# Moving the normalisation of the layer norms before the first feed-forward layer and the second attention from GpSimd to VectorE

## The reference

```
x = x + tanh(g_xattn[0]) * L0_xattn(layernorm(x), ctx, ...)   # 16 heads of 64
x = x + tanh(g_ffn[0])   * L0_ffn(layernorm(x), ...)          # 8 gated experts, dense
x = x + tanh(g_xattn[1]) * L1_xattn(layernorm(x), ctx, ...)   # 16 heads of 16
x = x + tanh(g_ffn[1])   * L1_ffn(layernorm(x), ...)          # top-2 of 8, only where routed
def _layernorm(x, eps=1e-05):
    m, v = mean(x, -1), var(x, -1)
    return (x - m) / sqrt(v + eps)
```

## Time and profile before

| | |
|---|---|
| median of 3 runs | 3753.66 us (3750.41 to 3754.77) |
| profiled execution, its own time | 3753.66 us |
| its span, first to last instruction | 3751.7 us |
| PE matmul busy | 3675.7 us (98% of the span) |
| DVE busy | 2420.4 us (65%) |
| ACT busy | 1707.0 us (46%) |
| POOL busy | 1508.2 us (40%) |
| granted TensorE clock, mean | 0.997 of full |
| POOL, normalising (L552) | 139.4 us in 256 instructions |
| DVE, y_minus (L1193) | 25.6 us in 128 instructions |

### The profile page before, as it was taken

The page is one execution under the profiler, slowest core; times in us unless marked ns, Lnnn a source line. Parts: engine busy times, 40 slices in busy tenths (PEclk is TensorE's granted clock), DMA queues, the critical chain, the costliest instruction groups (busy, mean ns, idle before and its releaser), DMA issues.

```text
span 3751.7 us, 96179 instructions
## 1 busy us (share of the span) xinstructions
PE 3675.7 (98%) x34836; PEld 2990.3 (80%) x34836; DVE 2420.4 (65%) x5566; ACT 1707.0 (46%) x3115; POOL 1508.2 (40%) x1589
## 2 busy tenths in 40 slices
PE   7999999999999999999999999999999999999998
PEld 5878878878878878878878878878878878878865
DVE  4566666666666666666666666666666666666675
ACT  4444444444444444444444444444444444444431
POOL 3434434434434434434434434434434434434433
PEclk9999999999999999999999999999999999999999
DMA  3000000000000000000000000000000000000001
GB/s 96 11 14 16 11 14 16 11 14 16 11 14 16 11 14 16 11 14 16 11 14 16 11 14 16 11 14 16 11 14 16 11 14 16 11 14 16 11 27 64
DMA packets 58916, 64.83 MB, mean 17 GB/s; under 512 B 5344, under 2 KB 55808, under 8 KB 58240
## 3 DMA queue, kind: packets, MB, share of 16 engines
q10 hardware_dynamic: 34688, 32.52, 2.9%
q1 hardware_dynamic: 24192, 31.81, 2.6%
HBM read 47.01 MB, written 17.30 MB: 17 GB/s over the span
## 4 chain that ended last, share of the span: by engine, by line
PE 77%; POOL 7%; DVE 7%; issue 5%; ACT 2%; POOLq 1%; DVEq 1%; SPq 0%; DMA 0%; ACTq 0%
PE g L834 24%; PE g L840 13%; PE scores L834 10%; PE g L987 6%; PE scores L937 6%; POOL q_lo L608 4%; PE g L1006 3%; PE g L903 3%; PE scores L997 3%; DVE y_nm L1269 3%; POOL kmx L601 2%; PE g L854 2%; PE scores L971 2%; PE scores L941 2%; PE g L914 1%
## 5 line engine op out<-in xcount | busy, mean ns | idle before, releaser
L777 ACT ACTIVATE prob<-scores 120x1024 f32<-120x1024 f32 x512 | 499.6, 1026 | 481.0 <-PE scores L941 444.1
L1330 DVE SCALAR_TENSOR_TENSOR x<-g,lg_w,x 128x256 f32<-128x256 f32 x1024 | 494.5, 483 | 259.9 <-PE g L834 236.1
L834 PE MATMUL g<-ew_hi,yT_hi 128*128 128x512 f32 x1024 | 428.1, 418 | 0.0
L543 POOL TENSOR_TENSOR y_rstd<-y_mv,eps 128x2 f32<-128x2 f32 x128 | 24.9, 195 | 970.5 <-DVE y_mv L1188 970.5
L613 POOL TENSOR_TENSOR q_lo<-an,q_hi 128x512 fp32r<-128x512 f32 x256 | 326.6, 1286 | 210.3 <-ACT q_hi L806 210.3
L834 PE MATMUL g<-ew_lo,yT_hi 128*128 128x512 f32 x1024 | 404.7, 395 | 0.0
L834 PE MATMUL g<-ew_hi,yT_lo 128*128 128x512 f32 x1024 | 404.1, 395 | 0.0
L1269 DVE TENSOR_REDUCE y_nm<-g 128x4 f32<-128x480 f32 x512 | 301.1, 651 | 110.1 <-PE g L914 110.1
L1269 DVE TENSOR_REDUCE x_nm<-g 128x4 f32<-128x480 f32 x512 | 312.4, 653 | 72.3 <-PE g L903 72.3
L543 POOL TENSOR_TENSOR x_rstd<-x_mv,eps 128x2 f32<-128x2 f32 x64 | 12.5, 196 | 835.7 <-DVE x_mv L1188 835.7
L608 POOL TENSOR_TENSOR q_lo<-q_full,q_hi 128x512 fp32r<-128x512 f32 x256 | 324.9, 1291 | 1.1 <-ACT q_full L711 1.1
(11 more groups left out here) (214 smaller groups left out, 9437.2 us busy)
## 6 DMA issues: line engine op xcount, KB each, us to landing
x_in<-in_x ACTq DMA_DIRECT2D x64, 256.0 KB, 2.9
out<-y_x SPq DMA_DIRECT2D x64, 256.0 KB, 2.1
ctx_in<-in_ctx ACTq DMA_DIRECT2D x128, 120.0 KB, 2.4
wk_s<-in_gu SPq DMA_DIRECT2D x8, 512.0 KB, 4.0
vx<-in_ew SPq DMA_DIRECT2D x2, 1024.0 KB, 5.0
wk_s<-in_wk SPq DMA_DIRECT2D x1, 1024.0 KB, 5.2
prob<-in_wq SPq DMA_DIRECT2D x1, 1024.0 KB, 7.7
wv_s<-in_wv SPq DMA_DIRECT2D x1, 1024.0 KB, 10.3
```

The source lines that it names most:

```text
L777: a.activation(prob[:, e].rearrange("p o u s -> p (o u s)"), scores[0:NK, banks, :].rearrange("p o c -> p (o c)"), ACT.Exp, scale=scale).t ...
L834: ins = t_.matmul(out_, lhsT[u], rhs[v], start=first and n == 1, stop=last and n == 3 * len(terms))
L1330: ins = v.scalar_tensor_tensor(out=x1[:, t, :], in0=ring.bank(Y_FFN[j])[:, o * D:(o + 1) * D], scalar=lg_w[:, t, 2 * n + o:2 * n + o + 1], ...
```

## The change

The two normalisations of the y family leave POOL. POOL keeps only add and power. DVE no longer computes y_minus (nor the drain before it), and two new DVE steps take over: p_norm, placed after y_maxt 1 and before n_q 2, and y_norm3, placed in the loop after x_mul 1 and before x_mul 2. Both wait for POOL's root and issue two tensor_scalar instructions (subtract mean, multiply by root), with the function that the next batch's layer norm uses. POOL's waits for the ring (that the earlier transposes of xn are over) go away; on DVE the order of its own steps covers them.

```
@@ ORDER (the ENDS lists get the same two steps in like places)
-    ("x_mul", 2), ("x_mul", 3), ("x_pv", 1), ("x_pv", 2), ("x_hi", 1), ("x_sum", 1), ("x_pv", 3),
+    ("y_norm3", 0), ("x_mul", 2), ("x_mul", 3), ("x_pv", 1), ("x_pv", 2), ("x_hi", 1), ("x_sum", 1), ("x_pv", 3),
-    ("y_maxt", 0), ("n_q", 0), ("n_k", 1), ("n_q", 1), ("y_maxt", 1), ("n_q", 2), ("p_load", 0),
+    ("y_maxt", 0), ("n_q", 0), ("n_k", 1), ("n_q", 1), ("y_maxt", 1), ("p_norm", 0), ("n_q", 2), ("p_load", 0),
@@ GpSimd
-            def rstd(mv, rs, stats, k_stats, done, k, i, minus=False):
+            def rstd(mv, rs, stats, k_stats, done, k, i):
-                if minus:
-                    stats.wait(pool, i, k_stats + 1)
-            def normalise():
-                pool.drain()
-                for t in range(T):
-                    ins = g.tensor_scalar(xn[:, t, :], x1[:, t, :], y_minus[:, t:t + 1], y_rstd[:, 1, t:t + 1],
-                                          ALU.add, ALU.mult)
-                ins.then_inc(y_normed.sem, 1)
             def y_norm2(i, _):
-                if not first(i):
-                    ring.full(pool, i - 1, Y_TR3)
-                rstd(y_mv, y_rstd, y_stats, 2, y_rs, 0, i, minus=True)
-                normalise()
+                rstd(y_mv, y_rstd, y_stats, 2, y_rs, 0, i)
             def y_stat3(i, _):
-                if not (isinstance(i, int) and i + 2 >= B):
-                    ring.full(pool, i + 2, X_TR)
-                rstd(y_mv, y_rstd, y_stats, 5, y_rs, 2, i, minus=True)
-                normalise()
+                rstd(y_mv, y_rstd, y_stats, 4, y_rs, 2, i)
@@ VectorE
-            def minus_mean():
-                dve.drain()
-                v.tensor_scalar(y_minus[:], y_mv[:, :, 0], -1.0, None, ALU.mult).then_inc(y_stats.sem, 1)
             def p_stat(i, _):
                 x_made.wait(dve, i, 1)
                 statistics(x1, y_st6, y_mv, y_stats)
-                minus_mean()
+            def p_norm(i, _):
+                y_rs.wait(dve, i, 2)
+                normalise(x1, y_mv, y_rstd, xn, y_normed)
             def y_stat3(i, _):
                 ring.all_empty(dve, i, Y_FFN[6:8])
                 statistics(x1, y_st6, y_mv, y_stats)
-                minus_mean()
+            def y_norm3(i, _):
+                y_rs.wait(dve, i, 4)
+                normalise(x1, y_mv, y_rstd, xn, y_normed)
```

More of the change, by code:

```diff
@@ L72 @@
         ("x_mul", 2), ("x_mul", 3), ("x_pv", 2), ("x_hi", 2), ("x_hi", 3), ("x_pv", 3), ("n_k", 0), ("n_tr", 0),
-        ("n_k", 1), ("x_out", 0), ("x_out", 1), ("x_out", 2), ("x_out", 3), ("p_stat", 0), ("n_q", 0),
+        ("n_k", 1), ("x_out", 0), ("x_out", 1), ("x_out", 2), ("x_out", 3), ("p_stat", 0), ("n_q", 0), ("p_norm", 0),
         ("n_q", 1), ("n_q", 2), ("p_tr2", 0), ("p_load", 0), ("n_q", 3), ("n_res", 0), ("n_max", 0), ("p_gate", 0),
@@ L80 @@
         ("x_st", 2), ("y_ffn", 3), ("n_norm", 0), ("y_ffn", 4), ("y_ffn", 5), ("y_ffn", 6), ("y_ffn", 7),
-        ("y_stat3", 0), ("n_tr", 0), ("x_pv", 0), ("x_sum", 0), ("x_mul", 0), ("x_st", 3), ("x_pv", 1),
+        ("y_stat3", 0), ("n_tr", 0), ("x_pv", 0), ("x_sum", 0), ("y_norm3", 0), ("x_mul", 0), ("x_st", 3), ("x_pv", 1),
         ("x_mul", 1), ("x_hi", 0), ("x_mul", 2), ("x_hi", 1), ("x_mul", 3), ("y_res", 0), ("x_sum", 1), ("x_pv", 2),
@@ L84 @@
         ("n_k", 0), ("n_v", 0), ("x_out", 0), ("y_max", 0), ("x_out", 1), ("x_out", 2), ("y_max", 1), ("x_out", 3),
-        ("p_stat", 0), ("n_q", 0), ("y_maxt", 0), ("n_k", 1), ("n_q", 1), ("y_maxt", 1), ("n_q", 2),
+        ("p_stat", 0), ("n_q", 0), ("y_maxt", 0), ("n_k", 1), ("n_q", 1), ("y_maxt", 1), ("n_q", 2), ("p_norm", 0),
         ("p_tr2", 0), ("n_q", 3), ("y_st", 0), ("n_max", 0), ("p_gate", 0), ("n_max", 1), ("y_st", 1), ("n_max", 2),
@@ L93 @@
         ("x_st", 2), ("y_ffn", 6), ("y_ffn", 7), ("y_stat3", 0), ("x_sum", 0), ("x_st", 3), ("x_pv", 0), ("m_coef", 2),
-        ("x_mul", 0), ("x_hi", 0), ("x_pv", 1), ("x_mul", 1), ("x_sum", 1), ("x_pv", 2), ("m_norm", 0),
+        ("x_mul", 0), ("x_hi", 0), ("x_pv", 1), ("x_mul", 1), ("x_sum", 1), ("x_pv", 2), ("m_norm", 0), ("y_norm3", 0),
         ("x_hi", 1), ("x_pv", 3), ("m_coef", 3), ("x_mul", 2), ("x_mul", 3), ("m_tr", 0), ("y_tr3", 0), ("z_out", 0),
@@ L97 @@
         ("y_res", 0), ("x_out", 1), ("x_out", 2), ("y_max", 1), ("x_out", 3), ("p_load", 0), ("p_stat", 0),
-        ("m_bias", 0), ("m_gu", 0), ("y_v", 0), ("p_ctx", 0), ("y_maxt", 0), ("y_maxt", 1), ("p_tr2", 0),
+        ("m_bias", 0), ("m_gu", 0), ("y_v", 0), ("p_ctx", 0), ("y_maxt", 0), ("y_maxt", 1), ("p_norm", 0), ("p_tr2", 0),
         ("p_gate", 0), ("y_st", 0), ("p_lg", 0), ("m_gu", 1), ("y_st", 1), ("y_mul", 0), ("y_pv", 0), ("p_wt", 0),
@@ L103 @@
         ("m_sig", 0), ("y_ffn", 0), ("y_ffn", 1), ("z_hi", 1), ("y_k", 0), ("y_ffn", 2), ("y_ffn", 3), ("m_sig", 1),
-        ("y_ffn", 4), ("y_ffn", 5), ("y_ffn", 6), ("y_ffn", 7), ("y_stat3", 0), ("m_gu", 2),
+        ("y_ffn", 4), ("y_ffn", 5), ("y_ffn", 6), ("y_ffn", 7), ("y_stat3", 0), ("y_norm3", 0), ("m_gu", 2),
         ("y_tr3", 0), ("m_sig", 2), ("z_out", 0), ("y_v", 0), ("m_dnw", 1), ("m_gu", 3), ("m_dnw", 0), ("y_q", 0),
@@ L312, in flamingo_stack @@
         y_st6, y_mv, y_rstd = sb("y_st6", [P, T, 6]), sb("y_mv", [P, T, 2]), sb("y_rstd", [P, 2, T])
-        y_minus = sb("y_minus", [P, T])
         yT = pair("yT", [P, KD, S])
@@ L356, in flamingo_stack @@
         x_attn_hi, x_attn_lo = signal("x_attn_hi", QUADS), signal("x_attn_lo", QUADS)
-        y_stats, y_rs, y_resd, y_normed = (signal("y_stats", 6), signal("y_rs", 4), signal("y_resd"),
+        y_stats, y_rs, y_resd, y_normed = (signal("y_stats", 4), signal("y_rs", 4), signal("y_resd"),
                                            signal("y_normed", 2))
@@ L1420, in m_gate_up @@
                 v.tensor_scalar(m_u[n % 2], m_u[n % 2], -LIMIT, 1.0, ALU.max, ALU.add).then_inc(m_up, 1)
-            run(dve, {"n_stat": n_stat, "n_norm": n_norm, "p_stat": p_stat, "y_stat3": y_stat3,
-                      "n_tr": x_tr, "n_k": x_k,
+            run(dve, {"n_stat": n_stat, "n_norm": n_norm, "p_stat": p_stat, "p_norm": p_norm, "y_stat3": y_stat3,
+                      "y_norm3": y_norm3, "n_tr": x_tr, "n_k": x_k,
                       "x_mul": x_mul, "y_mul": y_mul, "p_tr2": y_tr(Y_TR2, 1), "y_tr3": y_tr(Y_TR3, 3), "y_k": y_k, "y_q": y_q,
```

## The result

The changed kernel takes 3773.61 us (median of 4 runs, 3770.41 to 3775.9), the kernel before 3752.47 us (4 runs, 3750.41 to 3754.77): 1.0053 of the time before, interval 1.0041 to 1.0066. It is slower by 21 us, where 3728 was forecast. The span of the profiled execution grew from 3751.7 to 3772.6 us at a granted clock of 0.996, against 0.997.

What follows compares the result with a forecast made beforehand. PE's own stream was taken to bound the kernel, so only its stalls counted: 17.4 us (n_max 1) + 7.2 us (y_q) + 1 us (ends) = 25.6 us off 3753.66 us, giving 3728 us, range 3718 to 3748.

Steps and rivals of the forecast that it cites:

- the part on the lock: DVE and POOL exclude each other; L1197's 406 ns at half L1420's width taken as a slower mode, speaking for no contention.
- DVE, added: Two tensor_scalar per norm on DVE, at most 0.81 us a pair, none on PE's path; counted as 0 us.
- this rival: Lock, slower: p_norm held by q_lo 0 and kmx, PE stands 1.1 to 1.4 us at p_tr2; 3820 us, chance 0.08.
- signs of being wrong: A spread like L1420's, PE's transposes of xn waiting for DVE, or no turn shorter by 0.4 us though both waits are gone.
- p_stat, POOL: q_lo 0 starts 1.3 us earlier on POOL, so PE's 0.29 us stall at n_max 1 goes; worth 17.4 us.
- y_stat3, POOL: POOL's low halves come earlier, so yT_lo is ready and PE's 0.12 us stall at y_q goes; worth 7.2 us.
- Margin 0.7 us: At both y_norm3 and p_norm, xn would be ready on DVE 0.7 us before PE's transposes read it.
- the work of y_minus and the ring waits: Removing DVE's y_minus (25.6 us in 128) and drain, and POOL's ring waits, counted as nothing.
- The ends: First and last batches, where PE waited for xn itself: 2 us gained to 2 us lost, taken as 1 us gained.

Runs made afterwards that it cites:

- e6: The kernel before, with only n_norm of the x family cut into pieces of 128, 128, 64 and 192 columns instead of two of 256; 3751.85 us.
- e3: The changed kernel with p_norm put directly behind p_stat on DVE, ahead of kT_lo; 3805.41 us, 1.0141 of the kernel before.
- e4: The changed kernel with POOL waiting after each of the two roots until DVE has finished the norm; 3766.8 us, 1.0038 of the kernel before.
- e5: The changed kernel with p_norm directly behind p_stat and POOL waiting after each root for DVE's norm; 3721.96 us, 0.9919 of the kernel before.
- e7: The changed kernel with p_norm directly behind p_stat and POOL waiting for p_norm alone; 3716.2 us, 0.9909 of the kernel before.
- e1: The kernel before with only the norm of y_stat3 moved to DVE (y_norm3); 3742.82 us, 0.9974 of the kernel before.
- e8: The kernel before with only p_norm moved to DVE, directly behind p_stat, and POOL waiting for it; 3732.7 us, 0.9949 of the kernel before.
- e2: The kernel before with only p_norm moved to DVE, at the change's place; 3790.53 us, 1.0099 of the kernel before.
- e9: As e7, with y_norm3 one x_mul earlier, between x_mul 0 and x_mul 1; 3730.14 us, 0.9942 of the kernel before.

## Why the prediction failed

*The step that failed* is in the part on the lock: L1197 "looks like an instruction of another, slower mode", because it is half as wide as L1420 and takes nearly as long. In the sum this is the term "DVE, added", which put the new instructions at 0.81 us a pair and "none of it on PE's path": 0 us. Measured, it is 60 x 0.93 us at p_tr2 and 60 x 0.15 us at y_tr3, 65 us. A rate was read from one duration each. e6 shows that two thirds of these 406 ns are fixed and that the slope allows L1197 the rate of L1420's best. So the comparison of durations spoke neither for nor against the lock; L1420's spread, which was for the lock, should have decided, and with it the fact that p_norm was moved to where POOL has q_lo 0 and kmx without a break. A chance of 0.08 for this rival was much too low. That L1197 is free of the lock "is not shown" stood in the same paragraph. Two of the signs of being wrong that the prediction names came: a spread like L1420's, and PE waiting for DVE's xn.

*The lock.* In the Trainium skill (SBUF — State Buffer, Who interferes with whom) the rule is that whoever comes first has the shared ports for its whole instruction and the other is blocked; e3 agrees, where POOL is first by 0.07 us and the DVE pair takes 3.17 us instead of 0.74, and so does the change, where the first instruction of y_norm3 is ahead of q_lo by 0.22 us and takes its 0.40. How far POOL is blocked when it comes second is not settled: that q_lo begins 0.19 us before the norm's end and takes only 0.05 us more. In e4 and e5 the two never meet, and all norms take 402 to 417 ns. The same section says that an instruction with at most one input in SBUF, outside the modes that use both port pairs, does not contend; kT_lo agrees, with 0.66 us beside q_lo 0. No run here shows the ports themselves, only that the engines exclude each other for these two kinds of instruction.

*The size of that rival.* It had PE standing 1.1 to 1.4 us at p_tr2, 3820 us. The transposes came 0.93 us late. As it says, the first instruction gets in at the end of q_lo 0 and the second waits for kmx; but it let xn be ready 0.5 us or more after kmx (1876.3 against 1875.8), and it is 0.15 us. It spoke of p_norm alone; y_norm3 was held too, for 0.15 us a turn. And it credited the change with only 0.12 us a turn, though both stalls went: 0.60, and 0.19 elsewhere. Its condition, a delay of more than 1.1 us, was met: p_norm's pair took 1.57 us longer than the 0.74 us of an undisturbed one.

*p_stat, POOL.* Right. The stall at n_max 1 went from 0.494 to 0.204, 0.29 us, forecast 0.29, and ACT's wait for POOL disappeared.

*y_stat3, POOL.* Right in kind, wrong in size. The step to y_q fell by 0.31 us, not 0.12. I had taken 0.21 us, the distance from a score matmul to the maxima, for the distance between context transposes and y_q; unhindered it is 0.026.

*DVE, added.* "a pair takes at most 0.81 us": wrong at both places, 1.70 and 2.31 us, and right once POOL waits, 0.72 to 0.74 us. "Margin 0.7 us" was used up at both: 0.15 us late at y_tr3, 0.93 at p_tr2. Taking away the work of y_minus and the ring waits showed no cost of its own.

*The ends.* I had 1 us of gain. In the change the time before and after the turns grew by some 4 us (20.9 us of span, less 57 to 60 turns of 0.29), with the same norms held there.

*Would 3728 have come without the lock?* e5 has all of the change, p_norm earlier, the lock out of the way and POOL held for one norm each time: 3722. With e7 it is 3716. The forecast's gains were real: in e5 n_max 1 and y_q give 0.29 + 0.08 us a turn, 22 us where the sum had 24.6. Some 9 us of e5's 31 are the experts' matmuls, which the forecast didn't have; that e5 came so near to 3728 is in part luck. What the forecast missed was the price at p_tr2 and, smaller, at y_tr3.

*Open.* The gain at the experts' matmuls, some 0.15 us a turn, comes when both norms leave POOL: e1's gain of 10 and e8's of 18 make 28 us, and e7, which has both, gains 35. But the same kernels differ in another thing too. As long as a norm is left on POOL the program has the buffer y_minus, 8 bytes a partition, and it is declared directly before yT, which these matmuls read. In the five kernels with it (before, e1, e2, e6, e8) the matmuls of ew_hi with yT_lo are busy for 404.1 to 404.6 us, in the six without it (the change, e3, e4, e5, e7, e9) for 398.6 to 399.5 us. No run takes the buffer away alone or leaves it in alone, so whether the place of the buffers or the work of the engines does it is not shown. A form of the normalisation that DVE runs without meeting the lock (one input in PSUM, or another operation) was not tried.

## What to carry to other kernels

An instruction moved from one engine to another takes its neighbours from the new place: before adding its duration at a quiet place, look for what the other engine runs beside it, and at the spread (least, median, longest) of its kind wherever the two meet. If a kind ends a fixed, short time behind the other engine's instruction, it is held, and then it matters who starts first. The cure is an order, not less work: let the short one go first and the other engine wait for it, where the wait has cover (-57 us for e7 against the change, its earlier place included), and leave it held where the wait would cost more (e5 against e7). And never compare the rates of two instructions by one width of each; a piece of another width separates what is paid once from what is paid per column.

## What the runs showed of the hardware

- A DVE instruction of this kind beside POOL's low halves takes up to 1874 ns instead of 406 and ends 0.15 us after POOL's; POOL's loses little in the loop (kmx 1.83 against 1.79 us). Near the end of e8 one of POOL's own normalising instructions took 806 ns instead of 559 beside L1425 of DVE, which took its usual 426.
- Small leads decide who waits: POOL's lead of 0.07 us in e3 makes DVE's pair take 3.17 us; DVE's lead of 0.22 us at y_norm3 in the change leaves its first instruction at 0.40 us.
- The normalisation, with mean and root of each partition as its scalars, pays about 0.27 us once and 0.52 ns a column; L1420, with constants as scalars, would pay about 0.16 us once if its slope is the same, which was not measured.
- A change of one wait can shorten a program: e4 is the change with two waits more and takes 7 us less (the intervals just overlap).
- The same matmul of PE, same instruction and same shapes, took 395 ns in the five kernels with the buffer y_minus and 389 to 390 in the six without; the cause is open.
